# Cross-attention with the normalized queries written by GpSimd in place of VectorE

## The reference

```
x = x + attn(layernorm(x))
x = x + xattn(layernorm(x), ctx, ctx)        # this stage
x = x + ffn(layernorm(x))

def xattn(q, k, v):                          # 32 query heads, 8 key heads, 16 channels a head
    scores  = einsum('bkgsd,bktd->bkgst', qh, kh) / sqrt(16)
    weights = softmax(scores)                # over the 512 context tokens
    return einsum('bkgst,bktd->bkgsd', weights, vh)

def layernorm(x): return (x - mean(x)) / sqrt(var(x) + 1e-5)
```

## Time and profile before

| | |
|---|---|
| median of 3 runs | 1809.57 us (1806.09 to 1809.67) |
| span of the profiled execution | 1828.4 us, 18.8 us (1.0%) over the median; no time of its own beside the span is given |
| TensorE matmul busy | 1714.7 us, 94% |
| VectorE busy | 1210.7 us, 66% |
| ScalarE busy | 917.2 us, 50% |
| GpSimd busy | 183.6 us, 10% |
| cross-attention, by its items | from about 890 to 1280 us of the span |

### The profile page before, as it was taken

One profiled execution on the slowest core, in us unless ns is written; L12 is line 12 of the kernel. 1 busy time (PEld: TensorE's weight loads), 2 busy tenths in 40 slices (PEclk: granted clock), 3 DMA queues, 4 the chain that ended last, 5 costly groups with the idle time before them and its releaser, 6 DMA issues.

```text
span 1828.4 us, 26550 instructions
## 1 busy us (share of the span) xinstructions
PE 1714.7 (94%) x9753; PEld 1320.4 (72%) x9753; DVE 1210.7 (66%) x2477; ACT 917.2 (50%) x1937; POOL 183.6 (10%) x299
## 2 busy tenths in 40 slices
PE   5899999999999999998999999998995999999998
PEld 4788888888888888875533333333894999999997
DVE  6665766666655666667689999995541256666756
ACT  2544444444444444332477787877420146666641
POOL 1000000000000000020122322221106000000025
PEclk8999999999999999997799999999897999999999
DMA  4000000010000000022133344442104067887836
GB/s 150 1 1 12 24 24 1 1 35 1 24 1 24 12 24 1 1 59 68 45 96 89 123 141 134 132 135 66 50 13 184 1 231 266 299 273 275 294 122 228
DMA packets 103204, 167.21 MB, mean 91 GB/s; under 512 B 8325, under 2 KB 52357, under 8 KB 102309
## 3 DMA queue, kind: packets, MB, share of 16 engines
q1 hardware_dynamic: 97956, 148.74, 25.3%
q0 software_dynamic: 5120, 16.78, 2.7%
HBM read 116.15 MB, written 49.28 MB: 90 GB/s over the span
## 4 chain that ended last, share of the span: by engine, by line
PE 77%; DVE 16%; issue 3%; ACT 2%; another core or an unknown queue 1%; POOL 1%; DMA 0%; POOLq 0%; DVEq 0%; ACTq 0%
PE ps L189 38%; DVE xmax L1768 9%; PE ps L195 8%; PE ps L1436 7%; PE ps L1239 7%; PE ps L1131 6%; PE ps L1321 4%; PE ps L1192 3%; PE ps L1311 2%; DVE stats L206 1%; PE ps L1372 1%; DVE al L1783 1%; PE ps L1129 1%; ACT ah L1541 1%
## 5 line engine op out<-in xcount | busy, mean ns | idle before, releaser
L1768 DVE TENSOR_REDUCE xmax<-ps 128x1 f32<-128x512 f32 x512 | 320.7, 682 | 36.1 <-PE ps L1192 35.4
L1563 ACT ACTIVATE xp<-ps 128x512 f32<-128x512 f32 x512 | 273.1, 602 | 93.5 <-PE ps L1311 92.5
L1496 ACT ACTIVATE probs<-ps,nmax 128x128 f32<-128x128 f32 (+3 forms) x256 | 136.2, 532 | 164.5 <-DVE nmax L1736 164.5
L1192 PE MATMUL ps<-k,q 48*128 48x512 f32 x512 | 207.3, 483 | 7.4 <-DVE xmax L1768 4.7
L1311 PE MATMUL ps<-q,k 50*128 50x512 f32 x512 | 196.9, 467 | 6.0 <-ACT xp L1563 6.0
L1192 PEld LDWEIGHTS ps<-k,q 48*128 48x128 f32 x512 | 86.7, 193 | 144.7 <-DVE xmax L1768 115.0
L1536 ACT CAST pth<-ps 128x128 fp32r<-128x128 f32 (+3 forms) x256 | 108.5, 424 | 87.7 <-PE ps L195 87.7
L1321 PE MATMUL ps<-xp,vx 128*32 128x512 f32 x1024 | 140.3, 622 | 0.8 <-issue 0.8
L1736 DVE TENSOR_REDUCE nmax<-ps 128x1 f32<-128x128 f32 (+3 forms) x256 | 123.4, 482 | 14.9 <-PE ps L1131 13.5
L189 PE MATMUL ps<-w12h,x_h 128*128 128x352 f32 x568 | 121.6, 336 | 10.8 <-issue 10.3
L1775 DVE TENSOR_TENSOR ptl<-ps,pth 128x128 fp32r<-128x128 f32 (+3 forms) x256 | 123.8, 484 | 2.0 <-ACT pth L1536 2.0
(11 more groups left out here) (191 smaller groups left out, 3527.1 us busy)
## 6 DMA issues: line engine op xcount, KB each, us to landing
w_raw<-in_w_t SPq DMA_DIRECT2D x56, 704.0 KB, 5.9
w_raw<-in_w_t SPq DMA_DIRECT2D x28, 768.0 KB, 5.9
q<-q_way SPq DMA_DIRECT2D x64, 192.0 KB, 3.1
rows_x<-w_raw SPq DMA_DIRECT2D x39, 256.0 KB, 3.3
mixed<-rows_x SPq DMA_DIRECT2D x39, 256.0 KB, 4.3
rows_y<-y_s SPq DMA_DIRECT2D x39, 256.0 KB, 5.5
q_way<-q_hi SPq DMA_DIRECT2D x32, 256.0 KB, 4.2
w_raw<-in_w_qkv_t SPq DMA_DIRECT2D x24, 256.0 KB, 2.9
```

The source lines that it names most:

```text
L1192: pe.matmul(ps[:, bank, :], q3[rows, m % 4, h // 2, i * P:(i + 1) * P].bitcast(F32R), k3[rows, m % KV, :].bitcast(F32R), start=True, stop= ...
L1496: act.activation(probs[u % 4][:, 0:w], ps[:, S_BANK + u % 2, 0:w], ACT.Exp, bias=nmax[:, u % 4:u % 4 + 1], accum_out=rsum[:, u % 4:u % 4 + ...
L1563: act.activation(xp[:, m % 2, h, t, :], ps[:, XST + n % 3, :], ACT.Exp, scale=X_SCALE).then_inc(s_xe, 1)
L1768: dve.tensor_reduce(xmax[:, m % 2, h % 2, h // 2, i:i + 1], ps[:, bank, :], AX_X, ALU.max, negate=True).then_inc(s_xmax, 1)
```

## The change

The twelve query instructions of batches 1 to 3 leave VectorE's program and are put into GpSimd's, two at the end of item kv = 2 and two at the end of item kv = 3, behind `add_result`. VectorE gets one empty instruction (`nop`) behind the refinement of the roots, which raises the new semaphore `s_root`; the first query of a batch waits for that, and for the transposes of the batch before (`s_qt`), a wait that VectorE had. The queries of batch 0 stay on VectorE.

```diff
-QUERY_AT = [(2, 5), (2, 7), (3, 0), (3, 1)]
+QUERY_AT = {2: (0, 1), 3: (2, 3)}
...
                 if m >= 2:
                     add_result(m - 2)
+                if b + 1 < BATCH:
+                    for t in QUERY_AT.get(kv, ()):
+                        query(b + 1, t)
+
+            def query(b, t):
+
+                if t == 0:
+                    pool.wait_ge(s_root, b)
+                    pool.wait_ge(s_qt, KV // 2 * b)
+                src = res[:, b * TOK_TILES + t, :].rearrange("p (a j d) -> p a j d", d=XD, j=2 * XG)
+                pool.tensor_scalar(xn[:, t, :].rearrange("p (a d j) -> p a j d", d=XD, j=2 * XG), src, mv[:, t, 0:1],
+                                   rstd[:, t:t + 1], ALU.subtract, ALU.mult).then_inc(s_xn2, 1)
...
                 if (kv, k) == (2, 0):
                     roots(dve, count, norm, 0, TOK_TILES, s_pow, BATCH + 2 + b)
-                if (kv, k) in QUERY_AT:
-                    t = QUERY_AT.index((kv, k))
-                    if t == 0:
-                        dve.wait_ge(s_qt, KV // 2 * (b + 1))
-                    query(b + 1, t)
+                    dve.nop().then_inc(s_root, 1)
```

More of the change, by code:

```diff
@@ L485, in build @@
         s_xn2 = sem("s_xn2")
+        s_root = sem("s_root")
         s_cp = sem("s_cp")
```

## The result

The changed kernel took 1825.02 us (median of 6 runs, 1815.84 to 1833.11) against 1807.83 us before (6 runs, 1797.03 to 1811.37): a ratio of 1.0102, 95% interval 1.0065 to 1.014. Forecast were 1801.8 us and a range of 1799.0 to 1810.5. The change makes the kernel about 1% slower. Its six runs lie in two groups, 1815.84 to 1818.21 us at a mean granted clock of 0.962 to 0.963 and 1831.83 to 1833.11 us at 0.952 to 0.953, so that the median stands where no run does. The profiled execution took 1818.21 us itself, with a span of 1816.3 us; it is one of the shorter ones.

What follows compares the result with a forecast made beforehand. The prediction took VectorE as the bound in cross-attention items with queries, TensorE's own order in those without. From 1809.57 us, -5.21 (queries) - 2.56 (clock) + 0 + 0 = -7.77 us gave 1801.8 us; range 1799 to 1810.5.

Steps and rivals of the forecast that it cites:

- the price of a query on GpSimd: Queries in items kv = 2 and 3: 1.3 us each, a pair 2.6 of 2.85 us, so hidden.
- the row nearest in shape: The context's reordering on GpSimd, 512 elements, two inputs, heads and channels exchanged: 1304 ns, taken as the query's price.
- The formula behind it: Pair of queries of q us before the maxima split: hidden up to q = 1.43 us, above that delays it by 2q - 2.85.
- The scatter: GpSimd query's scattered write: slowed by VectorE's factor 1.43 (776 against 541 ns), it would bring the query to 1.87 us.
- The clock's step: Batch 1, behind TensorE's 1.2 us stop: the granted clock's fall costs 2.56 us, taken as gone if the long stops go.
- VectorE's queries: Twelve queries of batches 1 to 3 leaving VectorE: 1.73 + 1.72 + 1.76 = 5.21 us gained, without the clock.
- The window of 2.85 us: GpSimd, plain items: gap from the end of a result's addition to the next maxima split, 2.85 us.
- The empty instructions: Three on VectorE: between 0 and 0.2 us in all, covered by about 1 us of idle per item, taken at 0.
- the new waits: Waits on `s_root`, `s_qt` and for the consumer of `xn`: claimed not to bind, no cost.
- GpSimd's throughput: GpSimd is busy 3.5 us of an 11.56 us item, so throughput was claimed to be no question; the place is.
- slower: Rival: maxima split stuck behind GpSimd at six places, query 2.09 us, each pair 1.33 us late, 1814.9 us; chance 0.13.

Runs made afterwards that it cites:

- the middle pairs: Changed kernel with every GpSimd query in order with constants, mean, root and channel order left out (1926 ns each): 1810.1 us, ratio 1.0003 against before.
- the doses: GpSimd query pairs of different lengths in the changed kernel's places, first as six forms of the instruction in one kernel: one run, 1822.22 us.
- the pairs taken apart: Changed kernel with one query behind each addition and the two others behind the next maxima split, all on GpSimd: 1802.34 us, ratio 0.9963 against before.

## Why the prediction was wrong

**The step that failed is the price of a query on GpSimd.** The prediction took 1.3 us, "the row nearest in shape", with 0.53 and 1.87 us as bounds. It is 2.59 us, 0.72 us above the upper bound. The formula behind it was right in its form: a pair is hidden up to 2.85 us, and what is over delays the split and stops TensorE. In size it asks for a little too much, 2 x 2.594 - 2.85 = 2.34 us a pair where 2.07 us are measured (1.00 and 0.89 us for the middle pairs), since neighbouring instructions overlap in the profile: the pair spans 5.07 us, and the split starts 0.13 us before its end. With the measured 2.07 us the sum is -5.21 + 12.4 = +7.2 us, on the right side.

- The nearest row was that of another operation. The reordering of the context is a two-input product, and the prediction argued that one full input can't be dearer than two. The product takes 1.06 us in order and 1.19 us scattered; the operation with scalars takes 1.93 us in order with bare constants. The rows had no instruction of this operation at this size, so the honest upper end lay far higher than 1.87 us. (The 25% that the prediction gave for the permuting row, 1304 against 1058 ns, is 23%.)
- The scatter, which the prediction priced at a factor of 1.43 from VectorE's rows, is 0.13 us for the product and about 0.5 us here, factors of 1.12 and 1.26. It was overrated.
- The Trainium skill, "GPSIMD Engine Reference", section "Engine selection", calls one-input operations roughly line-rate. The runs disagree for this operation: in order and with both scalars it takes 2.08 us on GpSimd against 0.54 us on VectorE, and with constants 1.93 us against 1.06 us for GpSimd's two-input product. Its factor of 1.96 for an addition against VectorE (section "Performance versus the Vector engine") was nearer the mark, and still too low: 2594 against 776 ns is 3.3.

**The clock's step failed too, by its sign.** The 2.56 us were to be given back because "the long stops go". They did not go, they became longer: 2.39 us in place of 1.20. With them the clock fell more often and cost 12.6 and 25.4 us in two profiles. Even where the stops do go, as with the queries left out, 3.1 us of falls remain in batches 1 and 2, no less than the 2.5 us in before's profile. So the step was wrong in itself: the falls are not tied to that one stop.

**What held.** VectorE's queries cost 5.21 us: with them on no engine the time falls by 6.45 us, and the stretches come to the predicted 11.55 and 11.34 us. The window of 2.85 us is exact to a few hundredths in all the doses at full clock. The empty instructions and the new waits cost nothing that a stretch shows; in the kernel with the pairs taken apart, which has all of them, the stretches are those without queries. GpSimd's throughput is no question, only its place. The maxima on VectorE are not slowed, and the split takes at most 0.23 us in the changed kernel, where it took 0.63 us beside a query on VectorE.

**The rival that came true** is the one called slower: the split stuck behind GpSimd, decided from 1.86 us. It had the mechanism, the six places and the falls of the clock behind the stops, at 2.09 us a query and 1814.9 us. With 1816 to 1833 us the truth lies above even that. Its chance of 0.13 was too low for a case whose only point against it was a likeness between two operations.

## What to carry to other kernels

An instruction moved to an engine that has time costs nothing only if it fits into the gap at the place where it is put: measure the gap to the next instruction there that another engine waits for, and put the work behind that instruction, not ahead of it. Here the same twelve queries on the same engine are 6.1 us faster or 11.2 us slower than before, by their order alone. And take a price from a row of the same operation on the same engine; if there is none, the uncertainty is a factor and belongs in the range, however alike the shapes look.

## What was not expected of the hardware

On GpSimd the operation with scalars is slower than the product of two full inputs: 1934 ns with two constants against 1058 ns, for 512 elements per partition in order, and 2084 against 1190 ns where both do one arithmetic operation and write scattered. Reading a second full tile was cheaper here than naming a scalar.

The clock makes executions of one program differ. Beside the 14 us above, the part behind batch 3's items differs in length, 645.4 to 659.5 us over the eight profiles of changed kernels. In the changed kernel's profile, then in that without queries, the same part of the program (87 us from 112 us behind the end of batch 3's items):

```profile
1282.00:1369.00 87.00, 80.52 (x503) 63.33 (x504) 34.92 (x72) 41.79 (x67) 7.88 (x38) 0.89 0.16 52
```

```profile
1260.00:1347.00 87.00, 80.18 (x468) 59.99 (x465) 30.91 (x59) 37.66 (x61) 7.89 (x38) 0.81 0.16 52
```

At a mean clock of 0.89 TensorE did more of its work there (503 matmuls against 468), and the rest of the program is 646.6 us long in place of 652.9. Nothing in it was changed. A difference of 6 us between two single profiles of this kernel is thus no evidence for an edit; a stretch that is compared item by item at full clock is.

The 22.3 us of idle TensorE in before's profile stand in none of the other eight. They coincide with the experts' scatter transfers, which every execution has. Their cause stays open.
